# Expert rows added straight into the result, with an order kept by counts

## The reference

```python
def _moe(tokens, router_w, w1, b1, w2, b2):
    logits = tokens @ router_w.T
    probs = softmax(logits)
    rw, re = top_k(probs, 2)
    rw = rw / max(rw.sum(-1, keepdims=True), 1e-12)
    combine = zeros((N, E)).at[arange(N)[:, None], re].set(rw)
    out = tokens
    for e in range(E):
        h = gelu(tokens @ w1[e] + b1[e], approximate=False)
        y = h @ w2[e] + b2[e]
        out = out + combine[:, e:e + 1] * y
    return out

xn = layernorm(x)
x = x + gnn(xn, edge_index, edge_attr) + mix(xn)     # edge sums, an MLP of 512; attention
x = x + moe(layernorm(x))
```

## Time and profile before

| | |
|---|---|
| time, median of 3 runs | 1011.02 us (1009.95 to 1013.14) |
| the profiled execution's own time | 1009.32 us |
| its span in the trace | 1007.5 us |
| busy: PE / DVE / ACT / POOL | 857.4 / 647.1 / 411.4 / 697.2 us |
| mean granted TensorE clock | 0.916 |
| HBM read, written | 72.00 MB, 40.89 MB |

### The profile page before, as it was taken

The page is one execution under the profiler, slowest core; times in us unless marked ns, Lnnn a source line. Parts: engine busy times, 40 slices in busy tenths (PEclk is TensorE's granted clock), DMA queues, the critical chain, the costliest instruction groups (busy, mean ns, idle before and its releaser), DMA issues.

```text
span 1007.5 us, 19681 instructions
## 1 busy us (share of the span) xinstructions
PE 857.4 (85%) x6332; PEld 528.6 (52%) x6332; DVE 647.1 (64%) x2161; ACT 411.4 (41%) x1131; POOL 697.2 (69%) x503
## 2 busy tenths in 40 slices
PE   3778787988999999999999999999399952999920
PEld 2433433445445445544445555555289952899920
DVE  3699998996576365365455664656757873555524
ACT  3544653333454334334333443443144421676620
POOL 4788888888887878888778888887402668454420
PEclk7799998996999999999999999999799975999975
DMA  9865664545565555455535565434943424344459
GB/s 292 183 121 71 96 126 50 83 61 103 76 129 91 81 90 79 75 104 81 85 55 96 92 116 79 59 35 69 290 148 91 152 104 120 117 131 128 127 133 270
DMA packets 144169, 113.10 MB, mean 112 GB/s; under 512 B 106847, under 2 KB 129955, under 8 KB 143942
## 3 DMA queue, kind: packets, MB, share of 16 engines
q1 hardware_dynamic: 79988, 71.74, 25.6%
q0 software_dynamic: 56928, 25.42, 24.4%
q10 hardware_dynamic: 7154, 14.68, 4.7%
HBM read 72.00 MB, written 40.89 MB: 112 GB/s over the span
## 4 chain that ended last, share of the span: by engine, by line
PE 32%; POOL 14%; DMA 7%; DVE 5%; issue 5%; ACTq 0%; ACT 0%; SPq 0%; POOLq 0%; DVEq 0%
POOL edge_sums L695 13%; PE ps L1540 5%; PE ps L1551 5%; PE ps L1329 4%; PE ps L1469 3%; DMA edge_sums<-sums,addr 3%; DMA r2t<-expert_outputs 3%; PE ps L1136 2%; PE ps L1316 2%; PE ps L1265 2%; PE ps L1279 2%; PE ps L1459 2%; PE ps L1525 1%; POOL routed_rows L714 1%; DMA sums<-edge_sums 1%
## 5 line engine op out<-in xcount | busy, mean ns | idle before, releaser
L695 POOL DMA_INDIRECT edge_sums<-sums,addr x360 | 563.6, 1566 | 134.9 <-issue 107.0
L1692 DVE TENSOR_SCALAR oh<-node,dsrc 128x500 bf16<-128x500 int16 (+1 forms) x392 | 116.3, 358 | 73.4 <-PE ps L1329 73.0
L922 ACT ACTIVATE r<-ps 128x500 f32<-128x500 f32 (+1 forms) x224 | 103.4, 549 | 72.1 <-PE ps L1265 71.9
L1329 PE MATMUL ps<-oh,r2t 128*64 128x500 bf16 (+1 forms) x1176 | 130.7, 359 | 0.0
L1136 PE MATMUL ps<-edges,same 128*128 128x65 f32 x720 | 101.4, 287 | 11.3 <-ACT sums L755 4.6
L1655 DVE TENSOR_TENSOR r2t<-ps,r 125x4096 f32<-125x4096 f32 x25 | 110.3, 4412 | 0.0
L1136 PEld LDWEIGHTS ps<-edges,same 128*128 128x128 f32 x720 | 92.0, 200 | 33.8 <-issue 28.3
L1595 DVE SCALAR_TENSOR_TENSOR same<-srow,src_f,below 128x128 f32<-128x128 int32 x360 | 103.7, 345 | 4.1 <-DMA srow<-in_src_row 2.8
L1329 PEld LDWEIGHTS ps<-oh,r2t 128*64 128x64 bf16 x1176 | 59.0, 110 | 69.9 <-issue 39.2
L726 POOL DMA_INDIRECT expert_outputs<-r x56 | 54.4, 972 | 56.0 <-DVE r L2046 48.9
L1183 PE MATMUL ps<-r2t,r 125*32 125x512 f32 x400 | 59.3, 718 | 33.4 <-DVE r2t L1655 33.4
(11 more groups left out here) (280 smaller groups left out, 1379.5 us busy)
## 6 DMA issues: line engine op xcount, KB each, us to landing
srow<-in_src_row SPq DMA_DIRECT2D x45, 512.0 KB, 6.2
edges<-in_edge_attr SPq DMA_DIRECT2D x22, 512.0 KB
r<-routed_rows SPq DMA_DIRECT2D x56, 129.0 KB, 2.1
r<-hpre_rows SPq DMA_DIRECT2D x12, 500.0 KB, 4.3
edge_sums<-sums,addr POOLq DMA_INDIRECT x360, 3.2
r2t<-in_ew SPq DMA_DIRECT2D x4, 1024.0 KB, 9.4
hpre_rows<-r ACTq DMA_DIRECT2D x16, 250.0 KB, 2.2
edge_sums<-r SPq DMA_DIRECT2D x4, 884.0 KB, 13.4
```

Of the source, the lines that this page charges most:

```text
L695: pool.indirect_dma_start(out=tables[k], out_offset=bass.IndirectOffsetOnAxis(ap=addr[:, j:j + 1], axis=0), in_=sums[:, j % OR, :], in_off ...
L922: act.activation(phT[:, R % 2, h, 0:n], bank(BP[h], 128, 0, n), ACT.Square).then_inc(pair_squares, 1)
L1329: m = mm(ps[EA * a:EA * (a + 1), BD * BANK:BD * BANK + n], lhsT=parts3[:, (DCH - 1 - 2 * w // DW) * DW + (2 * w + a) % DW, s, :], rhs=oh[: ...
L1692: v.tensor_scalar(oh[:, (2 * i + a) % OHS, 0:nt * P].rearrange("p (t n) -> p t n", t=nt), node16[:, 0:nt, :], dsrc[:, 2 * w + a:2 * w + a ...
```

## The change

The result tensor `out` becomes the place into which the expert rows are added.

- ScalarE makes the residual row, x + normalised x, in `x_res` during the GNN stage, one activation for each tile (in `tok_copy`), with a scale and a bias that VectorE computes in two more small operations (in `xl_of`). SyncE stores these rows into `out` in six groups (`KEPT`) between its loads of `hpre`.
- GpSimd's scatter has `out` as its target and adds (`compute_op=ALU.add`); both choices of node n have index n. `youts`, the loads, the adds and the stores at the end are gone, and so are GpSimd's five residual adds.
- `out` gets 128 x 9 spare rows. Rows of padding are added into the first 128; idle steps read from rows of `routed` of their own and are added into spare rows of their own. SyncE and GpSimd set these rows early.
- Two adds to one row must not be in flight together. A node occurs once in one expert's rows, so only neighbouring steps of different experts can meet. GpSimd's scatter of step s waits for `may_add`, which SyncE raises in `allow(s)`: when the scatter of step s - 3 has landed, and that of step s - 1 too where a table `turn_i` says so; else the value waited for is one reached earlier. SyncE calls `allow(s)` behind its load of step s + 8 (`LEAD`).
- VectorE makes `turn_i` from the counts per expert after two of the batches (`CUTS`) and at the end (`turns`). Rows of an expert lie in the order of the batches; where the last tiles of one expert hold only late batches and the first tiles of the next only early ones, no strict wait is set.

```diff
@@ constants
+    KEPT = ((0, 4), (4, 8), (8, 12), (12, 17), (17, 22), (22, T))
+    BASE = 16
+    IDLE = E
+    SPARE = (0, 22, 44, 66, 88, 110, 128)
+    CUTS = ((1, 256.0), (2, 128.0))
+    LEAD = 8
@@ sync, behind the edge stage's loads
+            sp.wait_ge(consts, 25)
+            idle_rows = routed[E * REG:E * REG + 128 * IDLE, :].rearrange("(j p) f -> p j f", p=128)
+            sp.dma_start(idle_rows, pad_rows[:, :].unsqueeze(1).to_broadcast([128, IDLE, XF])).then_inc(pads_put, 16)
+            sp.dma_start(out[N + 128:N + 128 * (IDLE + 1), :].rearrange("(j p) c -> p j c", p=128),
+                         pad_rows[:, 0:C].unsqueeze(1).to_broadcast([128, IDLE, C])).then_inc(rows_kept, 16)
+            sp.wait_ge(pads_put, 16)
+            sp.dma_start(idle_rows[:, :, C + 1], idle_row[:, :], allow_slow_non_contiguous=True).then_inc(pads_put, 16)
@@ sync, GNN stage
+            def keep_rows(g):
+                t0, t1 = KEPT[g]
+                sp.wait_ge(rows_done, t1)
+                for a, z in PARTS:
+                    sp.dma_start(out[0:N, :].rearrange("(p t) c -> p t c", p=P)[a:z, t0:t1, :], x_res[a:z, t0:t1, :]
+                                 ).then_inc(rows_kept, 16)
             for i in range(2, NH2):
                 load_hpre(i)
+                for g, (t0, t1) in enumerate(KEPT):
+                    if t1 + 5 <= 2 * i <= t1 + 6:
+                        keep_rows(g)
+            for g, (t0, t1) in enumerate(KEPT):
+                if t1 + 5 > 2 * (NH2 - 1):
+                    keep_rows(g)
@@ sync, expert stage
                     sp.dma_start(xs[:, h, :], routed[bass.ds(row, 128), :]).then_inc(xs_loaded[h], 16)
+                    allow(s - LEAD)
+            def allow(s):
+                if s < 0:
+                    return
+                if s == 0:
+                    sp.wait_ge(rows_kept, 16 + 32 * len(KEPT))
+                    for k in range(SB):
+                        sp.wait_ge(ys_stored[k], BASE)
+                    sp.wait_ge(table_ready, 3)
+                else:
+                    turn = sp.value_load(turn_i[0:1, bass.ds(s, 1)], min_val=BASE, max_val=BASE + 16 * NS)
+                    sp.wait_ge(ys_stored[(s - 1) % SB], turn)
+                if s > 2:
+                    sp.wait_ge(ys_stored[(s - 3) % SB], BASE + 16 * ((s - 3) // SB + 1))
+                sp.sem_inc(may_add)
             steps(sp, load_steps, SB, 0)
+            for s in range(NS - LEAD, NS):
+                allow(s)
-            sp.wait_ge(residual, T // FT)
-            for g in range(T // FT):
-                for a, z in PARTS:
-                    sp.dma_start(outputs_of(g)[a:z, 0, :, :], youts[0:N, :]
...
@@ gpsimd
+            for k in range(SB):
+                pool.dma_start(out[N + SPARE[k]:N + SPARE[k + 1], :], pad_rows[SPARE[k]:SPARE[k + 1], 0:C]).then_inc(ys_stored[k], 16)
-            for g in range(T // FT):
-                xv = x_res[:, g * FT:(g + 1) * FT, :]
-                pool.tensor_tensor(xv, xv, xl_all[0:P, g * FT:(g + 1) * FT, 0:C], ALU.add).then_inc(residual, 1)
                     pool.wait_ge(ys_ready, s + 1)
                     pool.wait_ge(idx_ready, s + 1)
-                    pool.indirect_dma_start(out=youts, out_offset=bass.IndirectOffsetOnAxis(ap=y_idx[:, h:h + 1], axis=0),
-                                            in_=ys[:, h, :], in_offset=None, bounds_check=2 * N - 1, oob_is_err=False).then_inc(ys_stored[h], 16)
+                    pool.wait_ge(may_add, s + 1)
+                    pool.indirect_dma_start(out=out, out_offset=bass.IndirectOffsetOnAxis(ap=y_idx[:, h:h + 1], axis=0),
+                                            in_=ys[:, h, :], in_offset=None, compute_op=ALU.add).then_inc(ys_stored[h], 16)
@@ scalar, tok_copy
+                act.activation(x_res[:, t, :], x_res[:, t, :], ACT.Identity, bias=nmr[:, u, :], scale=rs1[:, u, :]).then_inc(rows_done, 1)
@@ scalar, end
-            act.wait_ge(residual, T // FT)
-            for g in range(T // FT):
-                for a, z in PARTS:
-                    act.dma_start(outputs_of(g)[a:z, 1, :, :], youts[N:2 * N, :]
...
@@ vector, xl_of
                 link(v.reciprocal(rs2[:, u, :], sd2[:, u, :]))
+                wait(v, rows_done, t - 1)
+                v.tensor_scalar(rs1[:, u, :], rs2[:, u, :], 1.0, None, ALU.add)
+                v.scalar_tensor_tensor(nmr[:, u, :], mv2[:, u, 0:1], -1.0, rs2[:, u, :], ALU.mult, ALU.mult)
@@ vector, expert stage
+            def turns():
+                link(v.memset(turn_m[:, NS:NS + 1], 0.0))
+                link(v.tensor_tensor(cut_ok, cut_n, e_pad[0:1, :].unsqueeze(1).to_broadcast([1, 2, E]), ALU.is_le))
...
+                link(v.tensor_reduce(turn_m[:, 0:NS], past[0:1, :, 0:E - 1], AX.X, ALU.max))
+                link(v.tensor_tensor(turn_m[:, 0:NS], turn_m[:, 0:NS], turn_m[:, 1:NS + 1], ALU.max))
+                v.wait_ge(consts, 24)
+                v.scalar_tensor_tensor(turn_i[:, 1:NS], turn_m[:, 1:NS], 16.0, turn_at[0:1, 0:NS - 1], ALU.mult, ALU.add).then_inc(table_ready, 1)
             for s in range(2):
                 w1_copy((s, s, 0), expert_of((s, s, 0)))
+            turns()
             steps(v, expert_steps, SB, 2)
-            for g in range(T // FT):
-                xv = x_res[:, g * FT:(g + 1) * FT, :]
-                v.wait_ge(node_rows[g], 32 + 64)
-                link(v.tensor_tensor(xv, xv, outputs_of(g)[:, 0, :, :], ALU.add))
-                v.tensor_tensor(xv, xv, outputs_of(g)[:, 1, :, :], ALU.add).then_inc(yb_added, 1)
```

More of the change, by code:

```diff
@@ L81, in gps_layer @@
         hpre_dram = nc.dram_tensor("hpre_rows", (128, MC, N), fp32, kind="Internal").ap()
-        routed = nc.dram_tensor("routed_rows", (E * REG + 128, XF), fp32, kind="Internal").ap()
-        youts = nc.dram_tensor("expert_outputs", (2 * N, C), fp32, kind="Internal").ap()
+        routed = nc.dram_tensor("routed_rows", (E * REG + 128 * IDLE, XF), fp32, kind="Internal").ap()
         x_res = sb("x_res", [P, T, C])
@@ L229, in gps_layer @@
         rs2 = carve([P, 2, 1])
+        rs1 = carve([P, 2, 1])
+        nmr = carve([P, 2, 1])
         lg = carve([P, T, E])
@@ L254, in gps_layer @@
         row_f = carve([128, NS])
+        cut_n = pasts[0:1, 0:2, :]
+        cut_ok = pasts[0:1, 2:4, :]
+        unsafe = pasts[0:1, 4, :]
+        turn_m = pasts[0:1, 5:5 + (NS + E) // E, :].rearrange("a s e -> a (s e)")
         places = carve([128, ND, T], bf16, at=at_u)
@@ L406, in gps_layer @@
         pads_put = sem("pads_put")
-        residual = sem("residual")
+        rows_done = sem("rows_done")
+        rows_kept = sem("rows_kept")
+        may_add = sem("may_add")
         table_ready = sem("table_ready")
@@ L1105, in _ @@
             steps(act, expert_steps, SB, 2)
-            for h in range(SB):
-                act.wait_ge(ys_stored[h], 16 * ((NS - h + SB - 1) // SB))
-            act.wait_ge(ey_ps, NS)
-            act.wait_ge(residual, T // FT)
-            for g in range(T // FT):
-                for a, z in PARTS:
-                    act.dma_start(outputs_of(g)[a:z, 1, :, :], youts[N:2 * N, :]
-                                 .rearrange("(p t) c -> p t c", p=P)[a:z, g * FT:(g + 1) * FT, :]).then_inc(node_rows[g], 16)
-            for g in range(1, T // FT, 2):
-                act.wait_ge(yb_added, g + 1)
-                for a, z in PARTS:
-                    act.dma_start(out.rearrange("(p t) c -> p t c", p=P)[a:z, g * FT:(g + 1) * FT, :],
-                                 x_res[a:z, g * FT:(g + 1) * FT, :]).then_inc(stored, 16)
         @program.tensor
@@ L1511, in _ @@
             pe.wait_ge(carried, len(BATCHES))
-            mm(bank(7, 128, 0, E), lhsT=ones[0:P, :], rhs=carry, start=True, stop=True).then_inc(ranks_ps, 1)
+            mm(bank(7, 128, 0, 3 * E), lhsT=ones[0:P, :], rhs=carries.rearrange("p a e -> p (a e)"), start=True, stop=True).then_inc(ranks_ps, 1)
             pe.wait_ge(table_ready, 2)
@@ L1960, in weights @@
                 v.tensor_copy(twin[:, :, C], runner[:, t0:t1])
-                v.tensor_scalar(twin[:, :, C + 1], dst_row[:, t0:t1], float(N), None, ALU.add)
+                v.tensor_copy(twin[:, :, C + 1], dst_row[:, t0:t1])
             def place(b):
@@ L1975, in place @@
                 v.wait_ge(carried, b + 1)
+                for at_, (cut_b, _) in enumerate(CUTS):
+                    if b == cut_b:
+                        v.tensor_copy(carries[:, 1 + at_, :], carry)
             link(v.memset(eps_col, LN_EPS))
@@ L2042, in output_rows @@
                 wait(v, xs_loaded[h], nth * 16 + 16)
-                wait(v, ys_stored[h], nth * 16)
+                wait(v, ys_stored[h], nth * 16 + (BASE if nth else 0))
                 v.wait_ge(tanh_ready, s + 1)
```

49 lines of the change are left out of this document (24 added, 25 removed).

## The result

The changed kernel takes 979.45 us at the median of 4 runs (973.49 to 983.50), beside 1010.49 (1007.58 to 1013.14) for the kernel before in the same series: a ratio of 0.969, 95% interval 0.963 to 0.975. Two more series of the same two kernels gave 0.9765 (0.9715 to 0.9815) and 0.9732 (0.9690 to 0.9774). Executions of one kernel scatter by some 5 us either way, and much of it comes from the edge stage: in the profiled runs of all kernels here the 300th edge scatter started at 584.3 to 592.6 us.

A forecast was written before the change was run, and what follows sets the result against it. The kernel was taken as a row of stages with different limits, ending in a DMA-bound tail. Terms 34.0 + 0.9 - 0.3 - 1.0 - 0.3 = 33.3 us saved from the 1011.02 median gave 977.7, range 972 to 991.

The forecast's parts named there:

- The tail goes: End of kernel: loads, ten adds and final stores vanish, only the last scatter's landing remains; 34.0 us earlier, bounds 31.6 to 35.8.
- From the last landing to the end of the program: Part of the new tail after the last scatter lands: between 0 and 1 us, 0.4 taken, new end 973.5.
- the sign that the prediction gave for being right: End of kernel: the span should end 4 to 6 us behind the last scatter's start.
- An adding row's DMA price: Expert-stage scatters: an adding 1 KB scatter takes 1.1 us of all DMA engines, against 0.34 for a plain one.
- SyncE: Expert-stage steps: added value load, waits and increment make SyncE's step 1.86 of 1.98 us, hidden behind TensorE.
- The rival that SyncE becomes the clock: Expert stage: SyncE's step reaches 2.1 to 2.4 us, total 983 to 998, TensorE waiting for tile loads; chance 0.11.
- Strict waits: Changes of expert: every change passes the table's tests, so only the wait three steps back remains, at no cost.
- The start gain of 0.9: Start of expert stage: without GpSimd's residual adds VectorE's weight copies are not stretched; 0.9 us gained, bounds 0 and 1.8.
- the prediction's two rules on VectorE and GpSimd: VectorE beside GpSimd: an add blocks it for the whole instruction; a scatter holds it up by only 0.3 us.
- Bursts of spare rows: Edge stage: SyncE's 2.1 MB of writes hold up the edge scatters by 1.0 us, bounds 0 and 4.
- one of the signs of being wrong: Edge stage: gaps over 1 us between edge scatters after 630 would show the forecast wrong.
- ScalarE's rows and the spare stores: Residual rows with VectorE's small operations delay routed scatters 0.3 us, at most 2.7; GpSimd's six small stores cost 0.3, at most 0.5.

## Why the prediction was right, and where it was off

It said 977.7 with a range of 972 to 991, and faster; it came out at 979.45, with 982.28 and 979.12 in the other series. The time was met more closely than the gain: 33.3 us were forecast, and the series show 31.0, 23.1 and, in the largest, 27.9 between their medians. The forecast started from 1011.02 for the kernel before, which took 1005.38 and 1006.97 in the two later series; that part of the agreement is luck.

- **The tail goes.** Right: no load of `expert_outputs`, and the end no longer moves with the full DMA engines. The last scatter was put at 969.4 on the clock of before, less the 0.9 gained at the start, 119.7 us behind the first transposes; it came at 119.6, and in five more runs at 119.4 to 119.9. The landing was 3.9 at the median, 3.7 predicted.
- **The step that failed** is "From the last landing to the end of the program: no row separates it. Between 0 and 1; 0.4 taken." It is 5.3 us (971.0 to 976.3), and the sign that the prediction gave for being right, an end 4 to 6 us behind the last scatter's start, did not come: it is 9.1. A row did separate it: the closing line of the kernel before in the trace, not among the rows shown ahead, was

```profile
L73 POOLq DRAIN  x1: 10660/10660/10660, 966.4 to 966.4; - x1
```

  That drain ended at 977.1, 9.95 us behind the start of GpSimd's last scatter, and was hidden beneath 30 us of tail. Taken over from there, the end would have stood at 969.4 + 9.95 = 979.4 instead of 973.5, and the sum at 27.4 us instead of 33.3; with the 9.1 measured it is 28.3.
- **An adding row's DMA price.** The 41 scatters of the window took 0.588 x 80/41 = 1.15 us of all engines, 1.1 predicted. By the rule of the Trainium skill ("Collectives: The Full Stack", Part 3, The bandwidth ceiling), that an add in the DMA path runs at half a copy's rate, which the page draws from the adds of a ring collective, it would have been 0.68, an estimate. Measured it is 3.4 times the 0.34 of a plain one, so the rule is too mild for these rows.
- **SyncE** needs 1.77 to 1.85 us a step, 1.86 predicted; a value load is 0.56, as predicted. The rival that SyncE becomes the clock comes true with one more load, but not by its sign: TensorE waits only 2.4 us for tile loads. VectorE's wait for a free result buffer, the likelier way, is not in the prediction.
- **Strict waits.** Right that none happens: SyncE waits 8.4 us in 9 waits for landings, and TensorE doesn't notice. The two kernels with more of them show what stood on that: 37 and 147 us.
- **The start gain of 0.9** stays open in size. The copies are short, as predicted; the line that answers to the earlier trace rows is

```profile
L2082 DVE COPY r<-r2t x56: 427/429/653, 836.9 to 957.4; 128x512 f32 x56
```

  The sixth tile's hidden layers came 1.3 us nearer to the first transposes in the first trace (11.99 instead of 13.29). Traces of the changed kernel differ there by 0.6, with the moment at which the clock rises, 5.0 to 6.3 us behind the first transposes. In the kernel before it rose at 6.1, and the five runs without the adds in which it rose at 6.3 to 6.5 have the sixth tile at 11.99 to 12.06, so at a like clock the start is 1.2 to 1.3 us shorter. With adds put back only 0.6 was lost, and none of it was left at the end; the adds' own share lies open between these. Of the prediction's two rules on VectorE and GpSimd the runs confirm what the rows had said: GpSimd's add shuts a copy out until it ends, as the Trainium skill has it ("SBUF — State Buffer", Who interferes with whom), while beside the adding scatters no copy took over 0.65 in the first trace and 0.77 in any.
- **Bursts of spare rows**: 1.3, 1.0 predicted; one of the signs of being wrong, a gap of over 1 us between edge scatters after 630, did come (2.19 at 634.97), within the bounds. **ScalarE's rows and the spare stores**, 0.3 each: from the last edge scatter to the last routed one it took 141.2 us before and 138.3 to 142.2 in the thirteen runs of this study, median 139.7; no loss is to be seen, and a gain of that size is within what the runs scatter. ScalarE's part by itself was not tried.

So the forecast is right by its main terms, and 4.9 us too good in one. The profiled execution, 978.03 us, came within some 2 us of its 976.0 because the first stretch, by chance, was 2.8 us better than its terms.

## What to carry to other kernels

When a change takes away what ends last, look up what each engine still had running under it, the closing drains too; the new end is the latest of those, not the last landing. An order kept by strict waits is priced by what queues behind the waiting engine: here a step with a strict wait lasts a landing and 0.7 us, and TensorE stands still while the tile loads are queued behind the permission and VectorE waits for a free result buffer; the test on the counts that avoids it was worth more than the tail. Before one more small instruction is given to an engine that feeds the bound one, add up its step: 0.13 to 0.21 us of slack per step were left, and a load of 0.56 cost 20 us.

## What the runs showed of the hardware

GpSimd's closing drain ends 7.3 us behind the end of its last work, whether that is an adding scatter of 1.54 us (8.85 behind its start in eleven runs) or a memset of 6.06 us with every scatter landed; where the program had two more waits behind its last scatter (without the idle steps' scatters) it was 7.5. In the kernel before, behind a plain scatter and beside full DMA engines, it was 9.0. What it spends the time on, and whether a GpSimd without indirect DMAs has it too, no run here shows.

An adding scatter of 128 rows takes GpSimd 1.54 us for rows of 1 KB and 1.55 for rows of 272 bytes, so between these two lengths the row's length doesn't matter to it; it does to the DMA engines, 1.15 us of all sixteen against 0.61.
